# Norm statistics woven between the links of a root's chain, three roots, late norms made in the loop, the router later

## The reference

```python
p = xn @ Wv.T + bv                     # 16 heads of 8 numbers
scores = p_head @ p_head.T / sqrt(8)   # query = key = value = p
s = softmax(scores) @ p_head -> merged @ Wo.T + bo

z = layernorm(xn) * ln_g + ln_b
probs = softmax(z @ rW + rb)           # 8 experts, the best two are kept
w = the two probabilities over their sum
mixed = sum over the two experts of w * (gelu(z @ W1[e] + b1[e]) @ W2[e] + b2[e])

out = x + s * silu(xn + mixed)
```

## Time and profile before

| | |
|---|---|
| median of three runs | 638.71 us |
| profiled execution | 637.87 us |
| its span, first to last instruction | 636.1 us |
| TensorE busy | 571.2 us (90%) |
| ScalarE busy | 542.5 us (85%) |
| VectorE busy | 244.5 us (38%) |
| granted TensorE clock, mean | 0.931 |

### The profile page before, as it was taken

One profiled execution on the slowest core, in us unless ns is written; L12 is line 12 of the kernel. 1 busy time (PEld: TensorE's weight loads), 2 busy tenths in 40 slices (PEclk: granted clock), 3 DMA queues, 4 the chain that ended last, 5 costly groups with the idle time before them and its releaser, 6 DMA issues.

```text
span 636.1 us, 11439 instructions
## 1 busy us (share of the span) xinstructions
PE 571.2 (90%) x3994; PEld 234.0 (37%) x3994; DVE 244.5 (38%) x709; ACT 542.5 (85%) x591; POOL 152.1 (24%) x170
## 2 busy tenths in 40 slices
PE   3666279999999999799999999999979999999995
PEld 2544033233434344333434444444433344433221
DVE  5673474772333333123222232223213663212463
ACT  5354146999999999999999999999998999999994
POOL 2334206777720000000000000000353700005760
PEclk9979555999999999879999999999986999999998
DMA  5117595767555554326454544453333756422230
GB/s 162 30 42 195 191 298 175 258 214 177 142 139 141 128 133 104 84 77 138 109 129 111 132 116 108 106 142 94 97 80 103 199 152 176 124 70 73 59 84 25
DMA packets 104059, 81.39 MB, mean 128 GB/s; under 512 B 51403, under 2 KB 95966, under 8 KB 103390
## 3 DMA queue, kind: packets, MB, share of 16 engines
q1 hardware_dynamic: 99902, 72.23, 42.7%
q0 software_dynamic: 4096, 8.40, 4.4%
HBM read 58.03 MB, written 28.32 MB: 136 GB/s over the span
## 4 chain that ended last, share of the span: by engine, by line
PE 66%; ACT 12%; DVE 8%; issue 5%; SPq 5%; DMA 2%; POOL 0%; ACTq 0%; DVEq 0%
PE bank_v L1238 32%; PE pair L1179 15%; ACT exps L712 9%; PE bank_f L1284 8%; PE bank_f L1275 7%; ACT pre L686 1%; PE bank_f L1255 1%; PE bank_f L1262 1%; DMA p_dram<-o_ring 1%; SPq L493 1%; DVE newton L736 1%; DVE rows_in_sb L746 1%; SPq L494 1%; DVE o_turned L992 1%; SPq L516 1%
## 5 line engine op out<-in xcount | busy, mean ns | idle before, releaser
L712 ACT ACTIVATE exps<-pair 128x1024 f32<-128x1024 f32 x512 | 488.1, 1052 | 47.6 <-PE pair L1179 29.8
L1238 PE MATMUL bank_v<-exps,v_tok 128*32 128x512 f32 x2048 | 282.4, 624 | 2.4 <-DVE o_turned L992 1.7
L1179 PE MATMUL pair<-q_ring,k_ring 26*128 26x512 f32 x1024 | 155.1, 510 | 11.9 <-ACT exps L712 9.9
L624 POOL DMA_INDIRECT rows_in_sb<-o_dram,dest_i x64 | 61.8, 966 | 375.5 <-DMA o_dram<-o_ring 342.8
L1179 PEld LDWEIGHTS pair<-q_ring,k_ring 26*128 26x128 f32 x1024 | 61.8, 186 | 107.2 <-ACT exps L712 66.1
L614 POOL DMA_INDIRECT z_dram<-pre,dest_i x64 | 63.6, 994 | 45.7 <-DVE dest_i L947 26.5
L1284 PEld LDWEIGHTS bank_f<-w_ring,pre 128*128 128x128 f32 x320 | 45.7, 206 | 71.4 <-issue 45.8
L1284 PE MATMUL bank_f<-w_ring,pre 128*128 128x128 f32 x320 | 61.9, 320 | 9.6 <-ACT pre L686 5.2
L1027 DVE TENSOR_TENSOR pre<-bank_f,w_ring 128x256 f32<-128x256 f32 x80 | 33.9, 423 | 94.5 <-PE bank_f L1275 94.5
L1275 PEld LDWEIGHTS bank_f<-zT,w_ring 128*128 128x128 f32 x320 | 41.7, 190 | 68.4 <-DVE pre L1027 46.8
L1238 PEld LDWEIGHTS bank_v<-exps,v_tok 128*32 128x32 f32 x2048 | 41.3, 110 | 69.3 <-ACT exps L712 38.3
(11 more groups left out here) (139 smaller groups left out, 281.7 us busy)
## 6 DMA issues: line engine op xcount, KB each, us to landing
w_ring<-w_dram SPq DMA_DIRECT2D x80, 192.0 KB
w_ring<-w_dram SPq DMA_DIRECT2D x80, 129.0 KB
q_ring<-p_dram SPq DMA_DIRECT2D x56, 104.0 KB
k_ring<-p_dram SPq DMA_DIRECT2D x56, 96.0 KB
z_dram<-s_tok SPq DMA_DIRECT2D x4, 1280.0 KB, 8.8
z_ring<-z_dram SPq DMA_DIRECT2D x80, 64.0 KB
o_dram<-o_ring SPq DMA_DIRECT2D x20, 256.0 KB, 2.4
p_dram<-z_ring SPq DMA_DIRECT2D x8, 256.0 KB, 2.9
```

What stands on the lines that cost most here:

```text
L624: pool.indirect_dma_start(rows_in_sb[:, (h * HT + i) % GATHER_RING, c, :], None, o_dram[h][:, :], bass.IndirectOffsetOnAxis(dest_i[:, h, c ...
L712: nc.scalar.activation(exps[:, g % ES, 2 * half:2 * half + 2, :], pair[(2 * g + half) % 3][:, :, :], ACT.Exp, scale=SCALE).then_inc(exp_do ...
L1179: ins = nc.tensor.matmul(pair[h % 3][:, j % 2, :], k_ring[32 * j:32 * j + KROWS, n % 2, kt * P:(kt + 1) * P], q_ring[32 * j:32 * j + KROWS ...
L1238: ins = nc.tensor.matmul(bank_v[32 * j:32 * j + 32, :], v_tok[:, (n // HG) * KT + kt, first:first + 32], exps[:, g % ES, j, :], start=(kt ...
```

## The change

Statistics of the first eight tiles come first; those of tiles 8 to 31 are issued one by one between two links of the gram sum and of the first two roots, before the wait of the link. There are three roots instead of five (8, 8 and 16 tiles), and the norm bound `m2` is reduced between two links of the first root. The gram sum has one operation less. The root of the second layer norm is taken once over all 32 tiles, after the fifth `keep_p`.

Only the norms of batches 0 and 1 are made in the prologue. Those of batches 2 to 7 are uses of `bank_f`, at steps 13 to 18; their buffer has two slots in another tile (`m_blk` is now in `w2_ring`), and VectorE waits for a slot's earlier store to land before it writes the slot again. SyncE stores each row one step after its use. If the bound asks for the exact path, these rows go to a spare row of `p_dram`: its number is computed by VectorE and loaded into a register of SyncE (`choose_m_row`). ScalarE no longer waits for the norm stores at steps 2 and 3.

The router of the first half moves from steps 0 to 12 to steps 2 to 14, the second half from 13 to 29 to 17 to 33; the exponentials from 2 and 15 to 10 and 21. The bias is made in eight uses instead of four. The second zeroing goes from SyncE's step 16 to step 12, the scatter of the halves from 6 and 22 to 11 and 31. The experts start one step later and are spaced by 1.08 steps instead of 1.12. x's first chunk is loaded ahead of Wv. `WARM` is 4 in both places, before 4 and 6. In `timetable()` both versions place 182 uses of `bank_f` at step 20 or later.

```diff
-NORMS = ((0, 4), (4, 4), (8, 8), (16, 8), (24, 8))
-WARM = (4, 6)
+NORMS = ((0, 8), (8, 8), (16, 16))
+WARM = (4, 4)
+EARLY = NB // B
...
-RANK_AT = ((0, 0, 1, 1, 2, 2), (13, 14, 15, 16, 18, 19))
-COUNT_AT = (3, 20)
-ASSIGN_AT = ((3, 4, 4, 5, 6), (21, 22, 23, 24, 26))
-SCALE_Z_AT = ((3, 4, 5, 6), (14, 15, 16, 18))
-EXP_AT = (2, 15)
-WEIGH_AT = ((10, 11, 12), (27, 28, 29))
+RANK_AT = ((2, 3, 3, 4, 4, 5), (17, 18, 19, 20, 22, 23))
+COUNT_AT = (7, 24)
+ASSIGN_AT = ((7, 8, 8, 9, 10), (25, 26, 27, 28, 30))
+SCALE_Z_AT = ((5, 6, 7, 8), (18, 20, 22, 23))
+EXP_AT = (10, 21)
+WEIGH_AT = ((12, 13, 14), (31, 32, 33))
 BIAS_AT = 4
-SCALE_W1_AT = (8, 10, 11, 12)
-SCATTER_AT = (6, 22)
-MOE_AT = 36
-MOE_STEP = 1.12
+BIAS_COLS = 2
+NORM_AT = 12
+ZERO_AT = 12
+SCALE_W1_AT = (13, 14, 15, 16)
+SCATTER_AT = (11, 31)
+MOE_AT = 37
+MOE_STEP = 1.08
...
+    for g in range(EARLY, NB):
+        place(("norm", g), NORM_AT + g - EARLY)
...
-        m_blk = exps[0:H, 2:4, :, :].rearrange("h a b n -> h (a b) n")
+        m_blk = w2_ring[:, :, :, :].rearrange("p a s f -> p (a s f)")[0:H, NB * BLK // 2:NB * BLK // 2 + 2 * BLK].rearrange("h (g n) -> h g n", g=2)
...
+            load_x(0)
             sp.dma_start(wv_sb, Wv).then_inc(wv_in, 16)
             sp.dma_start(bv_bc, bv.rearrange("(a d) -> a d", a=1).broadcast_to([P, D])).then_inc(wv_in, 16)
-            load_x(0)
...
-                if g == 2:
+                if g == EARLY:
+                    for e in range(EARLY):
+                        sp.wait_ge(n2_copied, e + 1)
+                        sp.dma_start(p_dram[:, M_ROW, e * BLK:(e + 1) * BLK], m_blk[:, e, :]).then_inc(m_kept[0], 16)
...
-                sp.wait_ge(n2_copied, g + 1)
-                sp.dma_start(p_dram[:, M_ROW, tokens], m_blk[:, g, :]).then_inc(m_kept[g // 4], 16)
...
+            sp.wait_ge(m_row_ready, 1)
+            m_row = sp.value_load(m_row_i[0:1, 0:1], min_val=M_ROW, max_val=SPARE_ROW)
+
+            def store_norms(g):
+
+                sp.wait_ge(bank_f_read, written("norm", g))
+                sp.dma_start(p_dram[:, bass.ds(m_row, 1), g * BLK:(g + 1) * BLK], m_blk[:, g % 2:g % 2 + 1, :]).then_inc(m_kept[1 + g % 2], 16)
...
+                if n == HG:
+                    for i in range(2):
+                        sp.wait_ge(m_kept[1 + i], (NB - EARLY) // 2 * 16)
...
-                if g == SCATTER_AT[1] - 6:
+                for e in range(EARLY, NB):
+                    if g == AT["norm", e] + 1:
+                        store_norms(e)
+                if g == ZERO_AT:
                     zero_z(1)
...
-                if 2 <= g < 4:
-                    act.wait_ge(m_kept[g - 2], NB // 2 * 16)
...
-            def link(ins):
+            def link(ins, beside=None):
+
                 links[0] += 1
                 ins.then_inc(dve_chain, 1)
-                dve.wait_ge(dve_chain, links[0])
+                at = links[0]
+                if beside is not None:
+                    beside()
+                dve.wait_ge(dve_chain, at)
...
+            def statistics():
+
+                t = next(tiles, None)
+                if t is None:
+                    return None
+                for chunk, (start, _) in enumerate(X_CHUNKS):
+                    if t == start:
+                        dve.wait_ge(x_in[chunk], 16)
+                return nc.vector.bn_stats(stats[:, t, :], x_tok[:, t, :])
+
+            def norm1(c, first, count, beside=None):
 
                 some = slice(first, first + count)
-                for t in range(count):
-                    for chunk, (start, _) in enumerate(X_CHUNKS):
-                        if first + t == start:
-                            dve.wait_ge(x_in[chunk], 16)
-                    ins = nc.vector.bn_stats(stats[:, t, :], x_tok[:, first + t, :])
+                for t in range(first, first + count):
+                    ins = nc.vector.bn_aggr(mv[:, t, :], stats[:, t, :])
                 link(ins)
...
-            norm1(0, *NORMS[0])
+            def beside_norm(c):
+
+                if c == 0 and links[0] == 7:
+                    keep_m2()
+                else:
+                    statistics()
+
+            for t in range(7):
+                statistics()
+            link(statistics())
             sum_gram()
-            norm1(1, *NORMS[1])
-            keep_m2()
+            norm1(0, *NORMS[0], lambda: beside_norm(0))
             router_weights()
+            norm1(1, *NORMS[1], statistics)
+            assert statistics() is None
+            keep_p(0)
             norm1(2, *NORMS[2])
-            keep_p(0)
-            norm1(3, *NORMS[3])
-            keep_p(1)
-            keep_p(2)
-            keep_n2(0)
-            norm1(4, *NORMS[4])
-            for g in range(3, NB):
+            for g in range(1, NB):
                 keep_p(g)
-                keep_n2(g - 2)
-            for g in range(NB - 2, NB):
-                keep_n2(g)
-            for h in range(HALVES):
-                norm2(h)
+                if g == 1:
+                    keep_n2(0)
+                elif g == 2:
+                    keep_n2(1)
+                elif g == 3:
+                    choose_m_row()
+                elif g == 4:
+                    norm2()
...
+                elif what == "norm":
+                    g = arg[0]
+                    if g < EARLY + 2:
+                        dve.wait_ge(m_kept[0], 16 * EARLY)
+                    else:
+                        dve.wait_ge(m_kept[1 + g % 2], (g - EARLY) // 2 * 16)
+                    ins = nc.vector.tensor_scalar(m_blk[:, g % 2, :].bitcast(F32R), bank_f[0:H, :], -1.0, None, ALU.mult)
...
-                    if s >= 3:
-                        norms_p(s - 3)
+                    if 2 <= s < 2 + EARLY:
+                        norms_p(s - 2)
...
                 first_scores(0)
                 rows_p(NB - 1)
-                norms_p(NB - 3)
                 first_scores(1)
-                norms_p(NB - 2)
                 first_scores(2)
-                norms_p(NB - 1)
...
+                elif what == "norm":
+                    pe.wait_ge(sq_ready, arg[0] + 1)
+                    ins = nc.tensor.matmul(bank_f[0:H, :], head_sel[:, :], sqT[:, arg[0], :], start=True, stop=True)
```

More of the change, by code:

```diff
@@ L136, in timetable @@
         place(("count", h), COUNT_AT[h])
-    for part in range(4):
+    for part in range(E * FC // BIAS_COLS):
         place(("bias", part), BIAS_AT + part)
+    for g in range(EARLY, NB):
+        place(("norm", g), NORM_AT + g - EARLY)
     t = MOE_AT
@@ L311, in build @@
         parts_stored = [sem(f"parts_stored{i}") for i in range(2)]
-        m_kept = [sem(f"m_kept{i}") for i in range(2)]
+        m_kept = [sem(f"m_kept{i}") for i in range(3)]
+        m_row_ready = sem("m_row_ready")
         m_zeroed = sem("m_zeroed")
@@ L731, in inverse_root @@
                 some = newton[:, 0:variance.shape[1]]
-                link(nc.vector.tensor_scalar(scale.bitcast(I32), variance.bitcast(I32), 1, None, ALU.logical_shift_right))
-                link(nc.vector.tensor_scalar(scale.bitcast(I32), scale.bitcast(I32), -1, RSQRT_SEED, ALU.mult, ALU.add))
+                link(nc.vector.tensor_scalar(scale.bitcast(I32), variance.bitcast(I32), 1, None, ALU.logical_shift_right), beside)
+                link(nc.vector.tensor_scalar(scale.bitcast(I32), scale.bitcast(I32), -1, RSQRT_SEED, ALU.mult, ALU.add), beside)
@@ L734, in inverse_root @@
                 for _ in range(NEWTON):
[L735 to L752 removed]
+                    link(nc.vector.scalar_tensor_tensor(out=some, in0=scale, scalar=-0.5, in1=scale, op0=ALU.mult, op1=ALU.mult), beside)
@@ new lines, in inverse_root @@
+                    link(nc.vector.tensor_tensor(some, some, variance, ALU.mult), beside)
+                    link(nc.vector.scalar_tensor_tensor(out=scale, in0=some, scalar=1.5, in1=scale, op0=ALU.add, op1=ALU.mult), beside)
+            tiles = iter(range(NT))
+            def statistics():
[6 more added lines that the diff above has]
+                return nc.vector.bn_stats(stats[:, t, :], x_tok[:, t, :])
@@ L753, in norm1 @@
+            def norm1(c, first, count, beside=None):
+                some = slice(first, first + count)
+                for t in range(first, first + count):
+                    ins = nc.vector.bn_aggr(mv[:, t, :], stats[:, t, :])
+                link(ins)
+                link(nc.vector.tensor_scalar(veps[:, some], mv[:, some, 1], EPS, None, ALU.add), beside)
+                inverse_root(veps[:, some], rstd[:, some], beside)
                 nc.vector.scalar_tensor_tensor(out=shift[:, some], in0=mv[:, some, 0], scalar=-1.0, in1=rstd[:, some],
@@ L1013, in read_bank @@
                 elif what == "bias":
-                    some = slice(arg[0] * 4, arg[0] * 4 + 4)
-                    ins = nc.vector.tensor_tensor(b1p[:, some], bank_f[:, 0:4], cols[:, some], ALU.add)
+                    some = slice(arg[0] * BIAS_COLS, (arg[0] + 1) * BIAS_COLS)
```

(3 more changed lines are left out.)

66 lines of the change are left out of this document (29 added, 37 removed).

## The result

The changed kernel takes 633.41 us (median of 4, 632.85 to 634.79), the kernel before 638.42 on the same chip: a ratio of 0.9917, 95% interval 0.9887 to 0.9946. That is 5.0 us less where some 13.7 were forecast. The profiled span fell from 636.1 to 633.1 us.

What follows compares the result with a forecast made beforehand. ScalarE's exponentials run near their floor, so only the start can give much. Profiled 637.87 us less 12.6 by step 20, 0 for steps 20 to 255 and 0.8 at the end: 624.5, median 625; 8 in 10 from 612 to 636.

Steps and rivals of the forecast that it cites:

- Start: Prologue: weight norm known at 11.7 us, first transposes at 17.6 instead of 21.6; 4 us won, bounds 0 and 5.
- Roots: Prologue roots: late batches' root ready near 29 us, first loads of heads near 40 instead of 48.12, bounds 37 and 45.
- Loop start: Start of the loop: first scores near 49.5 us, first exponential near 50.5, waits for squares and router gone.
- the two times given for step 15: Loop start: step 15 would come at 82 us, or at 95 with the low clock.
- Norms in the loop: Steps 13 to 18: VectorE waits for norm 2's row behind copies and second zeroing; norm 4 read near 104.5 us.
- After the wait: Steps 17 to 20: step 17 near 106.7 us, step 20 at 115.2 instead of 127.8; gain 12.6 us.
- just in time: Norm 7 waits for a row behind W1's 1 MB until about 114 us, in time for the turn of step 19.
- Steps 20 to 255: Rest of the loop: later start and closer spacing of expert products win nothing; 0 us, bounds -3 and 3.
- the windows for loads of weights stay at five steps or more: Expert steps: weight loads keep at least five steps, stated beside the 0 us taken for steps 20 to 255.
- SyncE's stretch does not move: Rival: copies stay at 88.8 us, step 20 comes at 124.5, whole 634.5 us; chance 0.12 (632 to 638).
- The clock stays low: Rival after the wait: steps take 2.6 us instead of 1.81, whole 645 us; chance 0.09 (640 to 648).
- The rows are not held: Rival on norm rows: other order on the engines or earlier bulk end, step 20 near 95, whole 605 us; chance 0.13.

Runs made afterwards that it cites:

- own_norm2: own_slots with the third inverse root moved behind the eight batches of rows on VectorE; 624.66 us, ratio 0.9789 to the kernel before.
- own_slots: The changed kernel with a place of its own in SBUF for each of the six late batches of norms; 623.67 us, ratio 0.977 to the kernel before.
- after_w2_turn: The changed kernel with W2's first two loads at steps 66 and 75 and z's loads and turns one step earlier; 629.45 us, ratio 0.983.
- w2_late: The changed kernel with W2's first two loads issued at steps 66 and 75 instead of 53 and 59; 632.15 us, ratio 0.9906.
- own_bias4: own_slots with four columns of bias in a part (BIAS_COLS = 4); 623.02 us, ratio 0.9761 to the kernel before.

## Why the prediction failed, step by step

*Start*: right. The weight norm was ready at 11.65 (11.7 forecast), the first transpose at 17.78 (17.6); the second came at 18.90, after 0.70 us for which the profile names no releaser (ScalarE's first eight tiles were ready at 17.44).

*Roots*: near. First loads at 40.77 (40).

*Loop start*: 2.2 us off, 52.7 for 50.5. I had not counted where the third root stands: between two batches of rows on VectorE, and TensorE waited 4.0 us for VectorE. In own_norm2, without that wait, the whole was no shorter. Of the two times given for step 15, 82 and 95 us, the one for the low clock came (95.31); it cost nothing here, since the wait for the row lasted longer.

*Norms in the loop*: right in mechanism and size. Copies issued at 80.13 (79.5), second zeroing behind them, read of norm 4 at 105.62 (104.5), step 17 at 107.7 (106.7). own_slots, with 12.3 us for 25.5, shows that the rows held these steps. The Trainium skill, "DMA: Bandwidth & Descriptors", section "Queues, rings and completion order", on which I leaned, says that a DMA engine takes the descriptors of a ring in order. The trace agrees: a 32 KB row issued at 92.56 was awaited until 105.6.

*After the wait*: 2.7 us off, step 20 at 117.9 for 115.2. I had norm 7's row land "just in time"; it cost a wait of 4.06 us.

*Steps 20 to 255*: the step that failed: 0 forecast with bounds of 3 on either side, 7.6 measured. I priced a use of bank_f wherever it stands, which held (2.07 us in after_w2_turn), and took what feeds the uses to have time, since "the windows for loads of weights stay at five steps or more". They were not at five steps even before: a load of W1 is issued one step after the last product that frees its ring place, and by the timetable four steps lie between load and use for quads 2, 5, 8 and 9 before and for 2, 3, 5, 6 and 9 after. Four steps are enough where nothing stands ahead (in w2_late step 64, four steps after its load, takes 2.07 us). For quad 6, whose load goes at step 60 in both, W2's load of some 4 us stands directly ahead, and the use moved from step 65 to 64: a wait of 0.18 us before became 2.38. Beside that, quads that begin at steps 42, 50 and 74 meet VectorE's turn of an attention block, one step in eight; before, only the one at 50 did. And at step 38 the first quad's turn came 0.4 us late, with z's first load behind the copies of W2. after_w2_turn moves all three: the six steps give back their 5.7 us, and steps 20 to 255 as a whole 4.8 of the 7.6. Of the 2.8 that are left (501.9 for 499.1), 1.2 are step 21 (3.29 us), ahead of the expert products, which fell into a stretch at the granted clock of 0.50 (118 to 122 us; 1.00 in the changed kernel). The rest, with no stretch above 1.0 us, stays open.

The rivals: "SyncE's stretch does not move" fell with the copies at 80.13; that the measured time lies in its range (632 to 638) is chance. "The clock stays low" fell as put: steps 20 to 37 took 31.1 us, 1.83 a step and not 2.6; what there was of it is step 65, 1.3 us longer, behind the wait at step 64. "The rows are not held" did not come, and own_slots shows that its 605 was priced too low: with nothing held, step 20 begins at 109 and not at 95, since steps 8 to 14 take 3.0 to 3.5 us each, at a granted clock of 0.50 until 98.

Had the term been taken as 5.7 us (the six steps), the forecast would have been 631; 2.7 us of the rest are the late step 20.

## What to carry to other kernels

When a timetable is drawn closer, don't count its uses alone: for each of them list what feeds it (queue, issue time, place in the queue, the engine's other periodic work) and compare with the new window, quad by quad. Look first for waits that are nearly nothing in the old trace (here 0.18 us): there the window has no slack left. A gain at the start is kept only as far as the serial queue behind it has slack; here, in own_bias4, 5.6 us gained by step 14 were lost again at step 38, behind SyncE's issues, which stand in one row up to 144 us. And give results that wait for a store their own places when memory is free: 9 us came from two corners of SBUF that nothing used at that time.

## What the runs showed that I had not expected

An issue on SyncE is not of fixed length. The two copies of W2 took 2.5 to 2.8 us to issue at step 33 in the runs with the changed start (3.9 in the kernel before) and 10.2 to 13.3 us at step 14, behind the copies inside p_dram and the second zeroing; the row of b1p took 0.57 us in the changed kernel and 2.6 to 6.1 in five of the runs with four bias columns. What stands behind such an issue on SyncE waits as long.

Links of the third root, 0.19 us each when GpSimd is idle, took 0.5 to 1.16 us while GpSimd was splitting a batch; all fourteen took 5.9 us in the changed kernel. The link of 1.16 us ended at 44.13, 0.05 us after an instruction of GpSimd, and from GpSimd's end at 45.07 on all links take 0.19.
